# Retention in groups, norms in halves with their gates inside, and four stages' weights requested one stage earlier

## The reference

```python
h = _L0_tok_ref(x, ...)
h = h + _L0_attn_ref(_layernorm(h), Wq, bq, Wk, bk, Wv, bv)   # retention, 12 heads of 16
h = h + _L0_ffn_ref(_layernorm(h), router_w, w1, w2)          # 16 experts, top 8
h = h + _L1_attn_ref(_layernorm(h), norm_w, norm_b, ...)      # a second norm, then Mamba
h = h + _L1_ffn_ref(_layernorm(h), Wr, ...)                   # 8 experts, top 2, one shared
h = h + _L2_attn_ref(_layernorm(h), w_qkv, ...)               # quantised attention
h = h + _L2_ffn_ref(_layernorm(h), P, C, ...)                 # codes
h = h + _L3_attn_ref(_layernorm(h), w_qkv, scale, ...)        # attention, top 75% of keys
h = h + _L3_ffn_ref(_layernorm(h), switch_w, ...)             # 8 experts, top 1
def _layernorm(x): return (x - mean(x)) / sqrt(var(x) + 1e-5)
```

## Time and profile before

| | us |
|---|---|
| three runs, median | 3777.4 (3774.78 to 3782.99) |
| the profiled execution, its own time | 3770.8 |
| its span in the trace | 3769.0 |
| busy: PE / DVE / ACT / POOL | 2575.4 / 2473.6 / 1558.3 / 896.6 |
| granted TensorE clock over the span | 0.821 of 2.4 GHz |

### The profile page before, as it was taken

One profiled execution on the slowest core, in us unless ns is written; L12 is line 12 of the kernel. 1 busy time (PEld: TensorE's weight loads), 2 busy tenths in 40 slices (PEclk: granted clock), 3 DMA queues, 4 the chain that ended last, 5 costly groups with the idle time before them and its releaser, 6 DMA issues. The chain is left out here.

```text
span 3769.0 us, 40855 instructions
## 1 busy us (share of the span) xinstructions
PE 2575.4 (68%) x13081; PEld 1601.0 (42%) x13128; DVE 2473.6 (66%) x5604; ACT 1558.3 (41%) x2778; POOL 896.6 (24%) x510
## 2 busy tenths in 40 slices
PE   2882799468888887569952112489889667776356
PEld 2772466323343433349941111233222256655345
DVE  4445233529999999611157998767877769999421
ACT  0000122146666674111113775477767535554211
POOL 2000000037767676147710000100000001111121
PEclk8775899779999998679975555799999888897578
DMA  1000200021102010051110000100000010000131
GB/s 35 7 7 21 93 0 0 2 72 45 69 22 90 13 78 0 1 164 40 37 45 0 1 1 1 53 1 1 1 1 1 1 29 1 1 1 1 46 119 50
DMA packets 59727, 108.45 MB, mean 29 GB/s; under 512 B 32253, under 2 KB 48091, under 8 KB 54331
## 3 DMA queue, kind: packets, MB, share of 16 engines
q1 hardware_dynamic: 53788, 94.44, 7.8%
q0 software_dynamic: 5760, 11.82, 1.0%
HBM read 92.17 MB, written 18.03 MB: 29 GB/s over the span
## 5 line engine op out<-in xcount | busy, mean ns | idle before, releaser
L1886 POOL TENSOR_TENSOR mam_st<-mam_du,mam_b_rows 128x1536 f32<-128x1536 f32 x128 | 439.6, 3441 | 171.5 <-PE mam_ysum L1955 170.9
L2116 DVE TENSOR_TENSOR_SCAN mam_st<-mam_da,mam_st 128x512 f32<-128x512 f32 x384 | 441.0, 1203 | 35.9 <-ACT mam_da L2056 18.2
L1651 DVE TENSOR_TENSOR cod_hp<-cod_hp,cod_gate 128x512 f32<-128x512 f32 x512 | 323.8, 680 | 122.4 <-ACT cod_hp L1518 120.4
L1955 PE MATMUL mam_ysum<-mam_st,held_ident 128*128 128x512 f32 x768 | 388.4, 646 | 2.2 <-DVE mam_st L2122 2.2
L1518 ACT ACTIVATE cod_hp<-cod_up,cod_b 128x512 f32<-128x512 f32 x512 | 319.2, 693 | 130.1 <-PE cod_up L1389 129.6
L2056 ACT ACTIVATE mam_da<-mam_delta,mam_decay 128x508 f32<-128x508 f32 x384 | 254.1, 683 | 184.2 <-DVE mam_st L2116 149.5
L471 DVE SCALAR_TENSOR_TENSOR held_h<-x_dn,held_gate,held_h 128x192 f32 x256 | 89.2, 410 | 225.3 <-PE x_dn L437 225.2
L2122 DVE TENSOR_TENSOR mam_st<-mam_st,mam_c_ps 128x1536 f32<-128x1536 f32 x128 | 224.4, 1753 | 16.7 <-PE mam_c_ps L1950 13.3
L1955 PEld LDWEIGHTS mam_ysum<-mam_st,held_ident 128*128 128x128 f32 x768 | 158.8, 207 | 167.3 <-issue 160.2
L312 POOL COPY held_xt<-n_cols 96x1024 f32 x32 | 34.5, 1082 | 773.9 <-ACT n_cols L293 773.9
L426 PE MATMUL x_up<-x_xg,x_w 96*128 96x512 f32 x384 | 177.5, 600 | 55.5 <-ACTq L451 55.5
(11 more groups left out here) (518 smaller groups left out, 5391.9 us busy)
## 6 DMA issues: line engine op xcount, KB each, us to landing
...
```

The source lines that it names most:

```text
L1651: nc.vector.tensor_tensor(at, at, gate[u % BANKS][:], ALU.mult).then_inc(gated, 1)
L1886: nc.gpsimd.tensor_tensor(st[it % N_ST][:], du[r % 2][:], along(b_rows[:, p % RING, n % PIECE, :], 1, [P, MC, MT]), ALU.mult)\
L1955: last = nc.tensor.matmul(ysum[:, c, :], m.ident[:], st[it % N_ST][:, c, :], start=False, stop=(it % DS == DS - 1))
L2116: nc.vector.tensor_tensor_scan(fs, fa, fs, 0.0, ALU.mult, ALU.add).then_inc(scanned, 1)
```

## The change

**Norms.** The 16 batches are handled in two halves of 8. DVE centres both halves, ACT squares them (it was DVE), and DVE makes the first half's scale and two of its four groups of rows before it sums the second half. The rows are made in place in `m.xn`; ACT writes the columns straight into `m.xt`; POOL has nothing left to do. The loops are written out. PE turns group g and then multiplies group g - 1 with the router.

On DVE, the middle of n0, before: one square and one sum over all batches, then the root's reciprocal.

```diff
-def norm_stage(nc, m, a, name, src=None, router=None, n_routes=0, affine=None, want_xn=False, add_src=False):
+def norm_stage(nc, m, a, name, src=None, router=None, n_routes=0, affine=None, add_src=False, ahead=(), gate=None):
...
+            for dst, array, done in ahead:
+                sp.dma_start(dst, a[array]).then_inc(done, 16)
...
+            def rows(g):
+                at = slice(g * GS, (g + 1) * GS)
+                x = m.xn[:, at]
+                last = nc.vector.tensor_tensor(x, x, along(rstd[:, at], 2, [P, GS, D]), ALU.mult)
...
+            for k in range(2):
+                centre(k)
+            for k in range(2):
+                spread(k)
+                scales(k)
...
+                for g in range(k * NG // 2, (k + 1) * NG // 2):
+                    rows(g)
+            if gate is not None:
...
+                c.step(nc.vector.memset(gate.work[:], 0.0))
                 for k in range(2):
...
+                    v.wait_ge(logits_kept, (k + 1) * NG // 2)
+                    gate.steps(nc, c, m, half(k))
...
+            for g in range(NG):
+                turn(g)
+                if router is not None and g:
+                    routes(g - 1)
...
+            def keep_cols(g):
+                act.wait_ge(turned_ready, g + 1)
+                nc.scalar.activation(m.xt[:, :, g * GT:(g + 1) * GT], turned[g % RING][0:DC], ACT.Copy)\
+                    .then_inc(cols_ready, 1)
...
+            for k in range(2):
+                act.wait_ge(centred, k + 1)
+                nc.scalar.activation(sq[:, half(k)], m.xn[:, half(k)], ACT.Square).then_inc(squared, 1)
+            root(0)
+            for g in range(NG):
+                if g == 1:
+                    root(1)
+                keep_cols(g)
+                if router is not None and g:
+                    keep_logits(g - 1)
...
-        @block.gpsimd
-        def _(pool):
-            with pool.Fori(0, NG // 2) as i:
-                for k in range(2):
-                    g = 2 * i + k
-                    if want_xn:
-                        pool.wait_ge(rows_ready[k], i + 1)
-                        nc.gpsimd.tensor_copy(m.xn[:, bass.ds(g * GS, GS), :], rows[k][:]).then_inc(rows_kept[k], 1)
-                    pool.wait_ge(cols_ready[k], i + 1)
-                    nc.gpsimd.tensor_copy(m.xt[:, :, bass.ds(g * GT, GT)], cols[k][:]).then_inc(cols_kept[k], 1)
...
-    c.step(nc.vector.tensor_tensor(work[1], others, own, ALU.is_equal))
-    c.step(nc.vector.tensor_tensor(work[1], work[1], along(tie, 1, shape), ALU.mult))
-    c.step(nc.vector.tensor_tensor(work[0], others, own, ALU.is_gt))
-    c.step(nc.vector.tensor_tensor(work[0], work[0], work[1], ALU.add))
-    c.step(nc.vector.tensor_reduce(rank, work[0], AX.X, ALU.add))
...
+    def rank_steps(self, nc, c, vals):
+        E = self.E
+        for e in range(E):
+            if e:
+                last = nc.vector.tensor_tensor(self.work[:, :, e, 0:e], vals[:, :, 0:e],
+                                               vals[:, :, e:e + 1].to_broadcast([P, self.n, e]), ALU.is_ge)
+            if e + 1 < E:
+                last = nc.vector.tensor_tensor(self.work[:, :, e, e + 1:E], vals[:, :, e + 1:E],
+                                               vals[:, :, e:e + 1].to_broadcast([P, self.n, E - 1 - e]), ALU.is_gt)
+        c.step(last)
+        c.step(nc.vector.tensor_reduce(self.rank[:], self.work[:], AX.X, ALU.add))
...
+RET_GROUPS = (4, 4, 4, 2, 2)
...
+            for b in range(NB):
+                scores(b)
+                if b - 1 in ends:
+                    means(ends.index(b - 1))
+                if b - 2 in ends:
+                    variances(ends.index(b - 2))
+                if b + 1 < NB:
                     projections(b + 1)
...
+                outputs(b)
+            means(len(ends) - 1)
+            variances(len(ends) - 1)
...
+            def keep_qk(b):
+                for dst, ps, bias, made, kept in ((q, q_ps, bq, q_made, q_kept), (k, k_ps, bk, k_made, k_kept)):
+                    act.wait_ge(made, b + 1)
+                    act.wait_ge(sc_ready, b)
+                    for g in range(HG):
+                        last = nc.scalar.activation(dst[:, g, :], ps[:, g * P:(g + 1) * P], ACT.Identity,
+                                                    bias=bias[:, g:g + 1])
+                    last.then_inc(kept, 1)
...
+            v.wait_ge(w_in, 128)
+            biased(0)
+            for b in range(NB):
+                decayed(b)
+                if b - 1 in ends:
+                    centre(ends.index(b - 1))
+                if b - 2 in ends:
+                    scaled(ends.index(b - 2))
+                if b - 4 in ends:
+                    add_back(ends.index(b - 4))
+                if b + 1 < NB:
+                    biased(b + 1)
+                gather(b)
+                if b in ends:
+                    sums(ends.index(b))
...
+        norm_stage(nc, m, a, "n1", router="L0_router", n_routes=16, gate=Gate(16, 8, True),
+                   ahead=((w1_sb[:], "L0_w1", w_in), (w2_sb[:], "L0_w2", w_in)))
+        experts_stage(nc, m, a, "x1", tiles, ACT.Gelu_apprx_tanh, w1_sb, w2_sb, w_in)
```

571 lines of the change are left out of this document (280 added, 291 removed).

## The result

The changed kernel took 3589.8 us (median of 4 runs, 3583.7 to 3593.0), the kernel before 3776.1 (4 runs, 3773.1 to 3783.0). The ratio is 0.950, with a 95% interval from 0.948 to 0.952: 186 us less, 26 us better than the forecast of 3616 and inside its range. The profiled execution took 3589.9 us with a span of 3588.0, against 3770.8 and 3769.0 before. So 181.0 of the 186 us can be looked up in the two traces, where the sum had 161.2. The other 5 come from the kernel before, whose profiled execution lay 5 us under this median; that of the changed kernel lies on its own.

What follows compares the result with a forecast made beforehand. No engine bounds the kernel; its time is the sum of what ends last in each stage. Savings of 45.4 + 24.0 + 36.0 + 55.8 = 161.2 us from 3777.4 give 3616, range 3580 to 3655.

Steps and rivals of the forecast that it cites:

- rival (a): Retention: the upper clock holds, q and k take 1.3 each, 33 us less, 3583; chance 0.20.
- Weights one stage earlier, 45.4: Starts of retention, experts, Mamba and attention: PE's wait for weights goes, 6.4 + 17.8 + 10.0 + 11.2 = 45.4 us saved.
- Rival (e): Loads: something on SP holds them, so they don't get hidden; 45 less saved, 3661; chance 0.04.
- Norms, 24.0: Norms n0, n2, n2b, n4, n5, n6: handled in halves, most end at about 24.3 us; 24.0 us saved in sum.
- The table's wait: Norms with a table load (1.3) between the squares and the first root: 0.7 us added.
- Norms with gates, 36.0: n1, n3, n7: gates start by halves inside their norms, with single comparisons for the rank; 15.5, 13 and 7.5 us saved.
- Rival (c): Gates: halves and comparisons dearer than priced, 20 to 30 us more, 3640; chance 0.15.
- Retention, 55.8: Retention: normalisation leaves every round, PE's scores wait for nothing; from 243.0 to 187.2 us, 55.8 saved.
- I keep the mix: Retention's round: PE's clock stays the mix of the kernel before, 10.5 us per batch.
- The tail: Retention's end: last round 6.5, last group's normalisation 7.0, way out and back 5.5, addition and barrier 1.4.
- Rival (b): Retention: clock falls to 1.2 GHz throughout, 12.8 us a round, 35 us more, 3651; chance 0.10.
- Rival (d): Retention: DVE waits mid-loop for a group's return, slower than before if 68 us per return; chance 0.01.

Runs made afterwards that it cites:

- one_piece: The changed kernel with every norm and gate in one piece of 16 batches instead of two halves of 8; 3611.2 us, ratio 0.958.
- wide_ranks: The changed kernel with the gates' ranks taken by four operations over all pairs, as in the kernel before, instead of single comparisons; 3607.4 us, ratio 0.956.
- wide128: The changed kernel with each output product of the retention streaming 128 columns instead of 16; 3568.3 us, ratio 0.946.
- kv_behind_outputs: The changed kernel with the next batch's kv product put between a batch's outputs and the next scores in the retention; 3641.4 us, ratio 0.964.

## Why the prediction was right, point by point

Two of the sum's four terms have a run that undoes them alone, the loads and the retention. No run puts the norms and gates of the kernel before back: their 68 us are read from the stages of the two traces, and one_piece and wide_ranks undo parts of them.

The mechanisms came as described, and the size of one term, the retention's round, was off. The total says less than it seems to: 3589.8 lies 26 us from the forecast and 7 from rival (a)'s 3583, though what (a) says, a clock that stays up, happened in four rounds of 15 only. That closeness is chance.

- **Weights one stage earlier, 45.4.** Right: 43.4 by the two traces, 48.6 in the trace without it. First PE instructions within 0.15 us of the stage's start and 1.2 in the experts, as was said. Mamba gave 7.9 for 10.0 in one comparison and 10.4 in the other, so the 2 us are within the spread of that stage. Rival (e) is out.
- **Norms, 24.0.** 29.2. Plain norms lie at 22.6 to 24.4, where 24 to 25 was said. In n4, n5 and n2b 0.7 us more were saved than priced, in n5 0.45 of it because DVE instructions with no wait between them overlap (1.76 long, 1.67 apart; 0.09 us at each of five places). n2 and n6 were better by 1.8 and 2.4: there the clock rose under the second turn (5.60 us of PE in the windows against 7.30 in n4 and n5), where the step took 1.94 per group at 1.2 GHz. n0 was worse by 1.1 for the same reason turned round: its turns took 7.29 us and not 5.60. The prediction misread n0's row here. It counted the 5.60 us as four turns at the full clock, but n2 and n6 have the same 5.60 with a clock that is low under the first two groups and up under the last two (3.65 and 1.95 us in n6); in n0 before, the first turns ran at the lower clock too. The table's wait was priced right, 0.91 us of idle time before the first reciprocal of n6 against 0.27 in n5. What the sum gave to the halves is in the main not theirs: in one piece n0, n4, n5 and n6 take 23.6 to 24.4 us all the same, and only in n5 and n6 do the halves show.
- **Norms with gates, 36.0.** 38.8: n1 17.6 for 15.5, n3 12.1 for 13, n7 9.1 for 7.5. The steps hold in n1. Its first half's logits were kept at 22.0 (22.5 was said), and a half of its gate took 13.8 (14.2) (timeline of DVE in n1):

```profile
259.07 0.29 DVE L373 TENSOR_REDUCE n_top_v<-held_logits 128x8 f32<-128x128 f32 x1 [0.95 <-ACT held_logits L313]
...
264.84 0.28 DVE L363 TENSOR_TENSOR n_work<-n_e 128x120 f32<-128x120 f32 x1
265.04 0.17 DVE L360 TENSOR_TENSOR n_work<-n_e 128x8 f32<-128x8 f32 x1
...
269.04 2.29 DVE L366 TENSOR_REDUCE n_rank<-n_work 128x128 f32<-128x2048 f32 x1
...
272.83 0.29 DVE L373 TENSOR_REDUCE n_top_v<-held_logits 128x8 f32<-128x128 f32 x1
```

  From 264.84 to 269.04 there are 30 comparisons, 0.14 apart, each 0.17 to 0.28 long. The second half starts at 272.83, with no wait for its logits. The prediction took 0.15, from a row in which two small instructions started 0.08 apart. The Trainium skill (VectorE: DVE Perf Modes, The TRN2 errata) has each pay a fixed latency, which by its fp32 formula would make 224 ns of a comparison of 64 elements, an estimate. The rows agree with such a length (0.17 for 8 elements, 0.28 for 120) and disagree with adding lengths up. Rival (c), comparisons and halves dearer than priced, is out by these rows.
- **Retention, 55.8.** 70.2, and the step that was off is a term of the sum, the round. "I keep the mix" took 10.48 us and 0.24 of averaging products; measured are 9.59 in the mean, 16.9 us less over the loop. What was mis-sized is the mix itself: it was taken from rounds in which PE stood for 3.1 us, all of them alike, and the new rounds are a few wholly fast ones among slow ones of 9 to 12 us. The mechanism was as described: PE waits for nothing but the sums at the start of a group's round (0.56), DVE is busy for 77 us of 173, and no instruction of DVE waits at `back_in` inside the loop. The tail took 23.1 us where 20.4 were counted (timeline of the retention's end, against the earlier trace rows):

```profile
217.05 5.28 PE L889 MATMUL ret_o_ps<-ret_kv,ret_ret 128*128 128x16 f32 x24 [1.92 <-DVE ret_var L992]
...
228.58 0.56 DVE L996 TENSOR_TENSOR ret_o<-ret_o,ret_inv 128x384 f32<-128x384 f32 x1
...
235.18 0.56 DVE L1000 TENSOR_TENSOR held_h<-held_h,ret_back 128x384 f32<-128x384 f32 x1 [5.57 <-DMA ret_back<-heads_scratch]
...
236.97 1.75 DVE L223 TENSOR_REDUCE n_runs<-held_h 128x96 f32<-128x1536 f32 x1 [1.24 <-PEq L73]
```

  The last outputs ran at 1.2 GHz after PE had stood for 1.92 us, 5.28 us instead of 2.75: that is nearly all of the difference. The way out and back took 6.0 us (5.5) and the last addition 0.56.
- **Rival (a), the upper clock holds, 3583.** Neither it nor the forecast was the truth: 4 rounds of 15 were wholly fast. Its argument, that PE has no idle time left, wasn't enough. The counter-argument, thin outputs, was the rest, and it took wide128 to show it: with hardly any idle time and 128 columns the clock holds and the loop is 7.7 to 8.6 us a round. The rival's own round of 8.3 was priced too high: it left the scores at 1.60, and they take 0.95 at the upper clock, so a wholly fast round is 7.63. The Trainium skill (TensorE: Matmul & The Clock Gate, Loop structure matters more than you think) has matmuls that follow one another stay warm. That is so in wide128 and not in the changed kernel, where twelve products of 16 columns follow one another as closely and the clock is 0.81 over the loop.
- **Rival (b), 1.2 GHz throughout, 12.8 a round,** didn't come, but kv_behind_outputs has 12.9 us in the mean: the same work in another order. That match is luck, since its clock is 0.58 and not 0.50. The rival's price was too low: it took the outputs at 3.2 us, and at the lower clock they take 5.14, so that a round throughout at 1.2 GHz is 14.7 to 15.1 us, which from the forecast's 10.5 is some 65 us more and not 35, outside the stated range.
- **Rival (d)** was never near: inside the loop each group was back before its turn.

Of the 26 us between forecast and result, 14.4 are the retention's, 5.4 the rest of the sum's (norms and gates up 8.0, loads down 2.0, untouched stages down 0.6), and 6.6 the kernel before's profiled execution, which was that far below the median the forecast started from and had no counterpart in the changed kernel.
